# Hybrid convolution, attention and recurrence: the last 16 keys' exponentials join the row sums on VectorE and GpSimd instead of TensorE

## The reference

```
dist2 = q2[:, :, None] + k2[:, None, :] - 2.0 * qk
scores = jnp.exp(-GAMMA * dist2)
attn = jax.nn.softmax(scores, axis=-1)
return jnp.einsum('bqk,bkd->bqd', attn, V)
```

## Time and profile before

| | us |
|---|---|
| median of 3 runs (224.82 to 226.02) | 224.94 |
| the profiled execution's own time | 225.0 |
| its span, first to last instruction | 223.1 |
| TensorE matmuls busy | 198.2 (89%) |
| ScalarE busy | 169.6 (76%) |
| VectorE busy | 161.1 (72%) |
| GpSimd busy | 28.7 (13%) |
| mean granted TensorE clock | 0.973 of full speed |

### The profile page before, as it was taken

How to read it: one execution, slowest core, us unless ns; L and a number is a source line. 1 busy time by engine, 2 the same in 40 slices (tenths; PEclk the granted TensorE clock), 3 DMA queues, 4 the chain that set the end, 5 groups by cost and what they waited for, 6 DMA issues and landing times. The chain is left out here.

```text
span 223.1 us, 3444 instructions
## 1 busy us (share of the span) xinstructions
PE 198.2 (89%) x1182; PEld 98.8 (44%) x1182; DVE 161.1 (72%) x294; ACT 169.6 (76%) x307; POOL 28.7 (13%) x44
## 2 busy tenths in 40 slices
PE   6976999999999969699799999999999998499960
PEld 6833646546546435223243343434343423276730
DVE  0449459999999944985876595959687794676980
ACT  4064599599799798979988989899999955465540
POOL 7000000370150080250001010101010000000000
PEclk9999999999999999969999999999999999889995
DMA  6940200295889494697805334260700000000016
GB/s 185 366 149 11 68 7 0 34 316 186 238 275 309 88 302 160 203 309 172 225 5 170 56 116 108 46 181 8 215 0 3 0 0 0 1 1 3 0 53 244
DMA packets 26885, 26.87 MB, mean 120 GB/s; under 512 B 1550, under 2 KB 25806, under 8 KB 26740
## 3 DMA queue, kind: packets, MB, share of 16 engines
q1 hardware_dynamic: 26868, 26.64, 40.3%
HBM read 14.74 MB, written 11.88 MB: 119 GB/s over the span
## 5 line engine op out<-in xcount | busy, mean ns | idle before, releaser
L510 ACT ACTIVATE arena<-ps 128x800 f32<-128x800 f32 (+1 forms) x56 | 44.4, 795 | 6.4 <-PE ps L1066 4.3
L517 ACT ACTIVATE arena<-arena 128x800 f32<-128x800 f32 (+1 forms) x56 | 46.3, 828 | 0.0
L1066 PE MATMUL ps<-qa,ka 128*128 128x400 bf16 (+1 forms) x128 | 35.5, 341 | 2.9 <-ACT arena L510 2.3
L1066 PE MATMUL ps<-qb,kb 96*128 96x400 bf16 (+1 forms) x128 | 35.3, 338 | 0.0
L742 DVE TENSOR_TENSOR psum<-arena 128x400 f32<-128x400 f32 x32 | 19.6, 611 | 13.4 <-ACT arena L517 13.4
L742 DVE TENSOR_TENSOR psum<-psum,arena 128x400 f32<-128x400 f32 x32 | 19.5, 609 | 7.7 <-ACT arena L517 6.3
L1066 PEld LDWEIGHTS ps<-qa,ka 128*128 128x128 bf16 (+1 forms) x128 | 10.4, 97 | 26.8 <-ACT arena L510 13.2
L1099 PE MATMUL ps<-arena,vb 128*32 128x400 f32 x192 | 21.6, 525 | 0.8 <-issue 0.7
L751 DVE RECIPROCAL arena<-ps 128x400 f32<-128x400 f32 x7 | 18.5, 2649 | 0.0
L661 DVE COPY arena<-arena 32x400 f32<-32x400 f32 x48 | 17.2, 358 | 0.9
L587 ACT ACTIVATE yb<-ps 128x160 f32<-128x160 f32 x36 | 10.9, 304 | 8.0 <-PE ps L1183 6.7
(11 more groups left out here) (148 smaller groups left out, 360.4 us busy)
## 6 DMA issues: line engine op xcount, KB each, us to landing
dka<-arena SPq DMA_DIRECT2D x16, 200.0 KB, 2.6
dqa<-arena SPq DMA_DIRECT2D x16, 200.0 KB, 2.5
ka<-dka SPq DMA_DIRECT2D x8, 400.0 KB
qa<-dqa SPq DMA_DIRECT2D x8, 400.0 KB
arena<-x_tok SPq DMA_DIRECT2D x4, 400.0 KB
t<-x SPq DMA_DIRECT2D x1, 1600.0 KB, 11.4
dkb<-arena SPq DMA_DIRECT2D x8, 200.0 KB, 2.7
dqb<-arena SPq DMA_DIRECT2D x8, 200.0 KB, 2.7
```

The lines of the kernel that those rows point to most:

```text
L510: nc.scalar.activation(prob[par][:, lo:hi, :], ps[:, o:o + hi - lo, 0:N], ACT.Exp, scale=2.0).then_inc(e1_done, 1)
L517: nc.scalar.activation(p, p, ACT.Exp).then_inc(p_ready, 1)
L1066: last = mm_(ps[row:row + keys, bank, 0:N], kk[par][0:rows, b, o:o + keys], qq[par][0:rows, b, :], start=first, stop=not first, skip_group ...
```

## The change

For groups 0 to 6 the product L1083 goes. In its place the tail rows of the last tile are added into the partial sums before `sums` reads them, one sample's 32 partitions at a time: samples 0 and 1 on GpSimd, samples 2 and 3 on VectorE. GpSimd first multiplies the 64 rows by a mask into `masked` (the first row of the output buffer, which is free then) and then adds twice; VectorE does mask and addition in one instruction each, with the mask as a per-partition scalar. The last group keeps the old way. Around it, `sums` moves from behind unit 3 to behind unit 4, the reciprocal from behind the additions of unit 2 to behind those of unit 3, and the quotient from unit 4 to unit 5 (in the last group from 2 to 3). GpSimd's loop over the pairs is written out, with `add_tails(g)` ahead of `values(g + 2)`. In the diff the first `add_tails` is GpSimd's, the second VectorE's.

```diff
+            def add_tails(g, par):
+
+                pool.wait_ge(vb_ready, min(g + 2, G))
+                pool.wait_ge(p_ready, UNITS * (g + 1))
+                rows = slice(0, C * POOL_TAILS)
+                nc.gpsimd.tensor_tensor(masked[rows, :], prob[par][rows, TILES - 1, :],
+                                        in_tail[rows, :].to_broadcast([C * POOL_TAILS, N]), ALU.mult).then_inc(masked_ready, 1)
+                pool.wait_ge(masked_ready, g + 1)
+                pool.wait_ge(part_sum, ADDS * (g + 1))
+                for b in range(POOL_TAILS):
+                    rows = slice(C * b, C * b + C)
+                    nc.gpsimd.tensor_tensor(psum[rows, par, b, :], psum[rows, par, b, :], masked[rows, :],
+                                            ALU.add).then_inc(tail_added, 1)
+                    pool.wait_ge(tail_added, POOL_TAILS * g + b + 1)
...
+            for g in range(G - 1):
+                add_tails(g, g % 2)
+                if g + 2 < G:
+                    pool.wait_ge(pv_done, g + 1)
+                    values(g + 2, g % 2)
...
+            def add_tails(g, par):
+
+                dve.wait_ge(p_ready, UNITS * (g + 1))
+                dve.wait_ge(part_sum, ADDS * (g + 1))
+                for b in range(POOL_TAILS, NB):
+                    rows = slice(C * b, C * b + C)
+                    nc.vector.scalar_tensor_tensor(out=psum[rows, par, b, :], in0=prob[par][rows, TILES - 1, :],
+                                                   scalar=c_("tail_ones")[rows, C * b:C * b + 1],
+                                                   in1=psum[rows, par, b, :],
+                                                   op0=ALU.mult, op1=ALU.add).then_inc(tail_added2, 1)
+
             def reciprocals(g, first=False):
-                dve.wait_ge(sums_done, g + 1)
+                dve.wait_ge(psum_used, g + 1)
...
                 if since > 1:
                     dve.wait_ge(psum_used, g - 1)
+                if since > 0:
+                    add_tails(g - 1, 1 - par)
                 for u in range(UNITS - 1):
                     add_tiles(g, par, u)
...
-                    if since > 0 and u == 2:
+                    if since > 0 and u == 3:
                         reciprocals(g - 1, first=since == 1)
...
-                    if since > 0 and u == (4 if g < G - 1 else 2):
+                    if since > 0 and u == (5 if g < G - 1 else 3):
                         quotient(g - 1, first=since == 1)
                         residual(g - 1)
...
-                pe.wait_ge(part_sum, ADDS * (g + 1))
+                if g < G - 1:
+                    pe.wait_ge(tail_added, POOL_TAILS * (g + 1))
+                    pe.wait_ge(tail_added2, (NB - POOL_TAILS) * (g + 1))
+                else:
+                    pe.wait_ge(part_sum, ADDS * G)
...
-                    if since > 0 and u == 3:
+                    if since > 0 and u == 4:
                         sums(g - 1, 1 - par, first=since == 1)
-                        tail_sums(g - 1, 1 - par)
```

More of the change, by code:

```diff
@@ L196, in build @@
         log_ready = sem("log_ready")
+        tail_added, tail_added2, masked_ready, mask_set = (
+            sem(n) for n in ("tail_added", "tail_added2", "masked_ready", "mask_set"))
         bn_c, bn_pe, bn_act, primed, cmp_c, cmp_pe, flag_ok, added = (
@@ L208, in build @@
         OUT_G = 2
+        POOL_TAILS = 2
+        masked = outs[:, 0, :]
+        in_tail = col(38)
         WARM_FIRST, WARM = 10, 2
@@ L392, in _ @@
                 square_parts(i)
[L394 to L398, removed]
+            def add_tails(g, par):
[11 more added lines that the diff above has]
+                    pool.wait_ge(tail_added, POOL_TAILS * g + b + 1)
+            pool.wait_ge(e_ready, PAIRS + CREDIT1)
+            for b in range(NB):
+                rows = slice(C * b, C * b + C)
+                nc.gpsimd.tensor_copy(in_tail[rows, :], c_("tail_ones")[rows, C * b:C * b + 1]).then_inc(mask_set, 1)
+                pool.wait_ge(mask_set, b + 1)
+            for g in range(G - 1):
[3 more added lines that the diff above has]
+                    values(g + 2, g % 2)
         @block.scalar
@@ L533, in last_reciprocals @@
             def last_reciprocals():
-                act.wait_ge(sums_done, G)
+                act.wait_ge(sums_done, 1)
                 act.wait_ge(nrm_ready, G - 1)
@@ L1076, in sums @@
                 for b in range(NB):
-                    last = mm_(ps[C * b:C * b + C, 5, 0:N], c_("ones"), psum[:, par, b, :], start=True, stop=False,
-                               skip_group_check=True)
+                    last = mm_(ps[C * b:C * b + C, 5, 0:N], c_("ones"), psum[:, par, b, :], start=True,
+                               stop=g < G - 1, skip_group_check=True)
                 last.then_inc(psum_used, 1)
```

## The result

The changed kernel takes 227.48 us (median of 20 runs, 225.04 to 229.62), against 225.04 us for the kernel before (20 runs, 223.84 to 227.37). The ratio is 1.0084, with a 95% interval from 1.0056 to 1.0113. It is slower by 0.8%, and the forecast was 227.2. Ratios here are taken over the executions within 1.5% of a kernel's fastest and medians over all of them, so the two can part by some tenths of a percent, most of all in experiment 7.

The account below looks back on a forecast made before the run. TensorE bounds the kernel before (12.00 of 12 us); after, the quotient's loop (12.1) and VectorE (12.2). First quotient +1.9 and five periods +0.8, with the end, make +2.1: 227.2 us, range 224.9 to 229.4.

Parts of the forecast that it names:

- the tight tie: In each group the quotient ends at 144.69 and TensorE's products waiting for it start at 144.79, nearly at once.
- The saving that does not arrive: Seven tail products, 5.5 us in all, leave TensorE, but it waits in front of the products for what it saved.
- The faster rival: Quotient's loop comes out at 11.3, so groups shrink by 0.7: 220.5 to 223.8 us, chance 0.12.
- The loop of 12.1: From one quotient's start through TensorE, ScalarE and VectorE to the next: 12.1 us a group, against 12.01 before.
- TensorE's way from the products to unit 6's scores: Loop step on TensorE: 9.27 us before, less 0.78 for the tail's product and some 0.1 for the sums: 8.4.
- Clashes at 0.64 each: VectorE loses 0.64 us for each GpSimd instruction beside it; three charged, 1.9 us a group.
- The sum of 12.2: VectorE's load a group, 10.3 us with two tails plus 1.9 for clashes: a second bound.
- The rival of the loop alone: No clash, since GpSimd works on two samples' rows only; quotients 12.1 apart: 226.2 us, chance 0.15.
- The rival of a harder saturation: VectorE clashes at 0.74 and tails at 0.65, 12.6 us a group: 229.5 us, chance 0.13.
- First quotient +1.9: Group 0's quotient starts at 110.0 instead of 108.12, with one clash with GpSimd of 0.5 us included.
- Five groups +0.8: Five periods between the quotients of groups 0 and 5 at 12.17 us each, against 12.01 before.
- a sign of being wrong: Sums that wait for GpSimd; GpSimd's tail rows were forecast to be in about 1 us before the sums.

Follow-up runs that it names:

- experiment 7: Changed kernel with reciprocal and quotient back at their old places and all four tails on VectorE, none on GpSimd: 225.74 us, ratio 0.996.
- experiment 10: Kernel before, full tail's product, with sums and tail's product moved earlier behind unit 2, reciprocal behind unit 1, quotient behind unit 3: 222.58 us, ratio 0.9878.
- experiment 1: Kernel before with only the three moves of sums, reciprocal and quotient; the tail's product stays on TensorE: 228.81 us, ratio 1.0167.
- experiment 3: Kernel before, old places, without the tail's product in groups 0 to 6 and nothing in its place: 223.1 us, ratio 0.9925.
- experiments 10 and 11: The second of these: kernel before with both the tail's product in bf16 and the earlier places of sums, reciprocal and quotient: 218.43 us, ratio 0.9673.
- experiment 2: Changed kernel without GpSimd's tail additions and TensorE's wait for them; tails of samples 0 and 1 missing from the sums: 228.06 us, ratio 1.0124.
- experiment 4: Changed kernel with all four tails on VectorE and none on GpSimd, places as changed: 228.17 us, ratio 1.0121.
- experiment 5: Changed kernel with all four tails on VectorE, plus 22 useless matmuls filling TensorE's first two gaps: 226.06 us, ratio 1.0052.
- 6: Changed kernel with reciprocal back behind unit 2 and quotient behind unit 4, tails still on both engines: 228.66 us, ratio 1.0164.
- 9: Kernel before, places unchanged, with the tail's product reading the upper bf16 halves of exponentials and ones: 223.77 us, ratio 0.9925.

## Why the prediction was right, point by point

**The bound before.** Right for the order as it stood: from 132.15 to 168.16 TensorE is idle for 0.03 of 36.01 us, and the tight tie costs some 0.1 us in every second group. What the prediction did not see is that TensorE's 12.0 us are not fixed: with the sums right behind a part of the products the same matmuls take 11.74 (experiment 10). At the first quotient the tie was already costing, 0.73 us.

**The saving that does not arrive.** Right, and shown twice: with the moves, TensorE waits 0.89 us a group for the quotient (experiment 1), and without the product at the old places only 2.3 of 5.5 us arrive (experiment 3). The faster rival was excluded by that. Over the earlier places, the saving of the product in bf16 arrives whole (11.74 to 11.15, experiments 10 and 11).

**The loop of 12.1.** Right in kind, too long by 0.15. Without clashes quotients are 11.95 apart (experiments 2, 4 and 5). The term that was too large is TensorE's way from the products to unit 6's scores. I had 8.4, with an estimate of 0.1 for the sums that no longer start behind scores; experiment 10 has 0.24 for such a move. In the changed kernel the way is 144.74 - 136.48 = 8.26:

```profile
136.48 0.88 PE L1141 MATMUL ps<-arena,vb 128*32 128x400 f32 x8 [1.43 <-issue]
...
144.74 0.36 PE L1104 MATMUL ps<-qa,ka 128*32 128x400 bf16 x4
```

**VectorE's load.** Tails at 0.60 were 0.65 (2.60 for four in experiment 7). Clashes at 0.64 each: tails take 1.3 instead of 0.65, the residual 0.73 or 1.27 by which engine comes first. That difference of 0.54 is the alternation of 11.94 and 12.46. The sum of 12.2 is what Q1 to Q5 give, 12.20. That GpSimd is on time in the steady state is right: its last addition ends at 151.83, and the sums start at 153.00. That clashes are a term of their own, and not only an excuse for the loop, is shown by 6 against 7: 0.69 us a group. For the changed kernel I put them at 109.26 - 108.06 = 1.2 us of its 1.70, by experiment 5, whose clock is at 1.00 in the same place; since that kernel also has filling matmuls and other tails, this split is an estimate. The rival of the loop alone gave 226.2, and experiment 5 measured 226.06 for much that case; but that rival has +1.2 us in the attention, and the trace of experiment 5 has +0.50, so the agreement is partly luck. The rival of a harder saturation did not come, but experiment 6 has its kind, 12.74 a group.

**The sum.** First quotient +1.9, measured +1.49. The place alone is worth 1.3 (P to Q0 is 24.70 in experiments 2 and 5, without GpSimd's tails; 1.4 by my numbers). The three additions ahead of the reciprocal did meet GpSimd, as I had charged (1.11, 1.21 and 1.05 us instead of about 0.57), but waits for exponentials there, which shrank, took most of it up: the clash cost 0.18 and not 0.5. Five groups +0.8, measured +0.70; of these 0.37 came in the first two distances, which are uneven before (10.92 and 13.12), and 0.33 in the three steady ones. The last group and the sums: -0.6 by my numbers, measured -0.50. Together +2.1, measured +1.70. The time moved by 2.44 in the medians and 0.84% in the ratio (1.9 us). That the median of 227.48 lies within 0.3 of 227.2 is therefore partly luck; the attention grew by 0.4 less than forecast.

**Missed.** In the first group GpSimd was late after all, which the prediction had named as a sign of being wrong. It copies its mask only after its earlier work (100.04 to 101.79), its additions end at 105.77, and TensorE waited for them:

```profile
105.82 0.88 PE L1119 MATMUL ps<-psum,cst 128*32 128x400 f32 x8 [1.22 <-POOL psum L410]
```

It had next to no consequence for the first quotient, 0.18 us with the clashes, as above; VectorE went from its additions into the reciprocal without a gap. Also missed: the half clock of experiments 1, 2 and 4. The changed kernel's profiled execution has none near 112 us, though TensorE was busy for only 2.28 of 4 us from 108 to 112. Whether some of its other executions have it, which would explain part of their spread from 225.04 to 229.62, stays open: only one execution has a trace.

## What to carry to other kernels

Before work is taken from the busiest engine, follow what the next group waits for once around all engines: where that loop is as long as the busiest engine's work, the saving turns into a wait, and what others wait for has to move ahead together with it (experiment 11 against 9). Count a new helper's cost on the engine that it clashes with, not only its own. Do not take a busy share of 12.00 of 12 for the least that the work can take: the order of the matmuls alone was worth 0.24 us a group. When a reordering is faster, split the gain into idle and busy time before naming its cause. Then look at the first group by itself, since one wait more there can cost clock as well as time.

## What the hardware showed that I had not expected

- GpSimd and VectorE clash even on different partitions: GpSimd's additions on partitions 0 to 31 and 32 to 63 and VectorE's tails on 64 to 95 and 96 to 127 took 1.25 and 1.3 us each; alone, a tail takes 0.65. The Trainium skill (SBUF — State Buffer, "Who interferes with whom") speaks of an exclusive lock and not of partitions; these rows agree with one lock for all of them.
- 32 partitions cost VectorE as much as 128: the scalar_tensor_tensor form took 0.63 us for a 32x400 tail (L774 in experiment 4) and 0.625 for 128x400.
- Order is time on TensorE: with bf16 scores between two float32 stretches the same matmuls took 3.96 us, and 3.72 with the float32 ones together (experiment 10).
- Two waits of TensorE close together (0.43 and 1.95 us in experiment 1, 1.49 and 1.65 in experiment 2, 1.21 and 1.92 in experiment 4) went with a granted clock of 0.64, 0.59 and 0.50 from 112 to 116, and that with its consequences cost 2.7 us in experiment 4 (against 5). The changed kernel has 0.14 and 1.65 us there and kept its clock. Ten and twelve matmuls without use in these waits kept the clock at 1.00.
- A float32 operand read as every second bf16 value made the product of 400 columns one instruction of 0.35 us, in place of two that the rows before show as 0.94. It is not the same product: weights and exponentials are cut to bf16.
